# Fourteen probability blocks turned as float16 on TensorE, their low halves turned in pairs by one DMA, value products two to three steps later

## The reference, cut to what matters

```
q = x W_q;  k, v = text W_k, text W_v;  k_ip, v_ip = ip W_k_ip, ip W_v_ip
p = softmax(q k^T / 4)                        # per head, 112 x 371
text_out = p v
qsem = p text;  qsem = qsem / |qsem|          # 512 wide
sem = qsem . (ip / |ip|)
p_ip = softmax(q k_ip^T / 4 + 0.5 sem) * mask
out = (text_out + p_ip v_ip) W_out + b_out + x
```

## Time and profile before

| | |
|---|---|
| runs shown | 740.36 us median (739.94 to 740.94) |
| the profiled execution | 739.64 us, its span 736.4 us |
| PE busy | 715.9 us (97%) |
| DVE busy | 634.7 us (86%) |
| ACT busy | 558.0 us (76%) |
| POOL busy | 416.9 us (57%) |
| DMA queue of SP | 64.39 MB, 41.3% of 16 engines' time |
| granted TensorE clock | 0.993 of full speed over the span |

### The profile page before, as it was taken

How to read it: one execution, slowest core, us unless ns; L and a number is a source line. 1 busy time by engine, 2 the same in 40 slices (tenths; PEclk the granted TensorE clock), 3 DMA queues, 4 the chain that set the end, 5 groups by cost and what they waited for, 6 DMA issues and landing times.

```text
span 736.4 us, 22506 instructions
## 1 busy us (share of the span) xinstructions
PE 715.9 (97%) x7215; PEld 562.2 (76%) x7215; DVE 634.7 (86%) x1878; ACT 558.0 (76%) x1591; POOL 416.9 (57%) x513
## 2 busy tenths in 40 slices
PE   7798999999999999999999999999999999999897
PEld 5477788787887878788787878878777887877664
DVE  4488998989889898988989898898989889898984
ACT  5378787887878788787878878787787878777770
POOL 7244647456564645656565555656555565654653
PEclk9999999999999999999999999999999999999999
DMA  9665363452636335263534526353352635234000
GB/s 283 125 163 105 78 129 78 64 130 55 125 75 125 82 61 140 46 126 74 111 98 62 124 55 131 75 115 93 58 115 72 127 75 106 51 56 102 10 7 16
DMA packets 137058, 68.56 MB, mean 93 GB/s; under 512 B 77056, under 2 KB 136880, under 8 KB 136944
## 3 DMA queue, kind: packets, MB, share of 16 engines
q1 hardware_dynamic: 132368, 64.39, 41.3%
q10 hardware_dynamic: 4576, 2.74, 1.4%
HBM read 40.38 MB, written 15.24 MB: 76 GB/s over the span
## 4 chain that ended last, share of the span: by engine, by line
PE 90%; DVE 3%; ACT 1%; DMA 1%; issue 1%; ACTq 1%; POOL 0%; SPq 0%; POOLq 0%; DVEq 0%
PE ps_prep L634 18%; PE ps_gram L741 18%; PE ps_pT L724 13%; PE ps_gram L742 12%; PE ps_score L716 6%; PE ps_prep L695 5%; PE ps_val L750 4%; PE ps_val L751 2%; PE ps_prep L692 1%; PE ps_prep L778 1%; PE ps_prep L665 1%; PE ps_prep L667 1%; PE ps_prep L789 1%; DMA w_raw<-in_L_xattn_W_k_ip 1%; PE ps_prep L782 1%
## 5 line engine op out<-in xcount | busy, mean ns | idle before, releaser
L564 POOL TENSOR_TENSOR dual<-prob 128x371 f32<-128x371 f32 (+1 forms) x288 | 251.0, 872 | 290.6 <-ACT prob L941 290.6
L741 PE MATMUL ps_gram<-gram_hi,pT_hi 125*128 125x371 f16 (+1 forms) x864 | 272.4, 320 | 0.1
L742 PE MATMUL ps_gram<-gram_lo,pT_hi 125*128 125x371 f16 (+2 forms) x864 | 230.1, 267 | 0.0
L935 ACT ACTIVATE pT_hi<-ps_pT 125x384 f16<-125x384 f32 (+1 forms) x288 | 138.8, 482 | 115.0 <-PE ps_pT L724 107.1
L1116 DVE TENSOR_TENSOR pT_lo<-ps_pT,pT_hi 125x384 f16<-125x384 f32 (+1 forms) x288 | 155.2, 539 | 31.8 <-ACT pT_hi L935 27.3
L925 ACT ACTIVATE prob<-ps_score,low 128x371 f32<-128x371 f32 (+1 forms) x288 | 165.4, 574 | 20.5 <-DVE low L1111 15.3
L1111 DVE TENSOR_REDUCE low<-ps_score 128x1 f32<-128x371 f32 (+1 forms) x288 | 154.9, 538 | 16.8 <-PE ps_score L716 11.7
L1129 DVE CUSTOM_DVE_ANT_0 quad_junk<-ps_gram,dual 128x371 f32<-128x371 f32 (+1 forms) x288 | 153.1, 532 | 3.6 <-PE ps_gram L742 0.8
L750 PE MATMUL ps_val<-val,pT_hi 125*128 125x84 f16 (+3 forms) x864 | 152.3, 196 | 0.0
L941 ACT ACTIVATE prob<-prob 128x371 f16<-128x371 f32 (+1 forms) x288 | 151.5, 526 | 0.0
L724 PE MATMUL ps_pT<-ident,prob 128*125 128x128 f32 (+1 forms) x864 | 142.0, 273 | 7.7 <-ACT prob L925 4.0
(11 more groups left out here) (214 smaller groups left out, 1466.8 us busy)
## 6 DMA issues: line engine op xcount, KB each, us to landing
ctx_sb<-in_ctx_t SPq DMA_DIRECT2D x15, 750.0 KB, 4.9
w_raw<-k_bounce SPq DMA_DIRECT2D x32, 216.0 KB, 3.9
k_st<-k_bounce SPq DMA_DIRECT2D x28, 216.0 KB, 3.8
k_bounce<-k_hi SPq DMA_DIRECT2D x15, 288.0 KB, 4.3
k_bounce<-k_lo SPq DMA_DIRECT2D x15, 288.0 KB, 4.3
q_st<-q_bounce SPq DMA_DIRECT2D x60, 63.0 KB, 2.4
xt_sb<-in_x_t SPq DMA_DIRECT2D x16, 168.0 KB, 5.3
k_st<-k_hi SPq DMA_DIRECT2D x32, 84.0 KB, 3.2
```

Source lines behind the costliest of these rows:

```text
L564: nc.gpsimd.tensor_tensor(dual[0:r, t % 2, :], prob[0:r, g % 4, 0:TX], prob_16[0:r, t % 2, :], ALU.subtract).then_inc(s_dual, 1)
L741: nc.tensor.matmul(ps_gram[t % 2][:, 0:TX], hi, gh[0:TROWS[i], i, :], start=(i == 0), stop=False, skip_group_check=True)
L742: last = nc.tensor.matmul(ps_gram[t % 2][:, i * TC:TX], hi, gl[0:TROWS[i], i, i * TC:TX], start=False, stop=(i == NT - 1), skip_group_chec ...
```

## The change

Blocks 0 to 13 (t < `NBX`) are treated in another way; blocks 14 to 17 stay as they were, but for where they are stored.

1. ACT writes prob_16 = float16(prob), not half of it, one block earlier and ahead of `pT_hi` (block t+2 at the start of step t), into four slots.
2. PE turns `prob_16` with the float16 identity into a float16 view of `ps_pT`; ACT copies it out as `pT_hi`, now with five slots. DVE's `pT_lo` of these blocks is gone.
3. POOL makes `prob_lo` = prob - prob_16 as float16 in SBUF, unturned, for block t+2. For each pair of blocks SP issues one transposing DMA of 128x768 float16 (`turn_lo`) into `turned_lo`, three slots.
4. `dual` is made by POOL (prob + prob_lo) for odd blocks below 14 and for 14 to 17, and by DVE (2 prob - prob_16) for even blocks below 14.
5. Gram products of block t stay in step t. Value products are made in pairs: blocks 2q and 2q+1 in step 2q+3, blocks 12 to 15 in step 15, 16 and 17 in their own steps. The copies out of `ps_val`, the moving of the cut heads' rows (SP, steps 14 and 15 to 16 and 17) and the end of the batch before (two steps later) follow.

```
-            nc.gpsimd.tensor_tensor(dual[0:r, t % 2, :], prob[0:r, g % 4, 0:TX], prob_16[0:r, t % 2, :], ALU.subtract)
+VALUES_AT = {**{2 * q + 3: (2 * q, 2 * q + 1) for q in range(6)}, 15: (12, 13, 14, 15), 16: (16,), 17: (17,)}
+HI_SLOTS, X_SLOTS, LO_PAIRS, TURNED_PAIRS = 5, 4, 2, 3
+def dual_on_pool(t):
+    return t >= NBX or t % 2 == 1
+    def turn_lo(b, q):                                       # SP
+        n = pair(b, 2 * q)
+        sp.wait_ge(s_prob_lo, lows_to(b, 2 * q + 1))
+        if n >= TURNED_PAIRS:
+            past = n - TURNED_PAIRS
+            sp.wait_ge(s_val, NB * (past // PAIRS) + 2 * (past % PAIRS) + 2)
+        sp.dma_start_transpose(turned_lo[:, n % TURNED_PAIRS, :, :],
+                               prob_lo[:, n % LO_PAIRS, :, :, :].rearrange("s a c t -> s (a c t)")).then_inc(s_turned[n % TURNED_PAIRS], 16)
                 for t in range(NB):                          # SP's loop
+                    if t % 2 and t < NBX - 2:
+                        turn_lo(b, (t + 1) // 2)
+                    if prepare and t == NB - 1:
+                        turn_lo(b.next(), 0)
+    def low_probs(b, t):                                     # POOL
+        pool.wait_ge(s_prob_16, g + 1)
+        nc.gpsimd.tensor_tensor(prob_lo[:, n % LO_PAIRS, t % 2, :, 0:TC], chunks(prob[:, g % 4, :]), chunks(prob_16[:, g % X_SLOTS, :]), ALU.subtract)
     def transposes(b, t):                                    # PE
+        if t < NBX:
+            pe.wait_ge(s_prob_16, g + 1)
+            src, out_, unit = prob_16[0:r, g % X_SLOTS, :], ps_pT[:, :].bitcast(F16), ident_16
+    def value_products(b, t):                                # PE
+            if t % 2 == 0:
+                pe.wait_ge(s_turned[n % TURNED_PAIRS], 16 * (n // TURNED_PAIRS + 1))
+            lo = turned_lo[:, n % TURNED_PAIRS, t % 2 * NT:(t % 2 + 1) * NT, :]
-                    products(b, t)
+                    gram_products(b, t)
+                    for u in VALUES_AT.get(t, ()):
+                        value_products(b, u)
-            probs_lo(b, t + 1)                               # DVE
+            duals(b, t + 1)      # even blocks below 14; probs_lo for blocks 14 to 17
-MOVE_OUT_STEP, MOVE_IN_STEP = 14, 15
+MOVE_OUT_STEP, MOVE_IN_STEP = 16, 17
```

More of the change, by code:

```diff
@@ L107, in column, with duals_to, pair, lows_to @@
     return (t - GROUPS[group(t)][0]) * BW
+def dual_on_pool(t):
+    return t >= NBX or t % 2 == 1
+def duals_to(b, t):
+    own = sum(dual_on_pool(u) == dual_on_pool(t) for u in range(NB))
+    return own * b.n + sum(dual_on_pool(u) == dual_on_pool(t) for u in range(t + 1))
+def pair(b, t):
+    return PAIRS * b.n + t // 2
+def lows_to(b, t):
+    return NBX * b.n + t + 1
+def old_lows_to(b, t):
+    return (NB - NBX) * b.n + t - NBX + 1
+def block_of(g):
+    return Batch(g // NB, g // NB % 2, g // NB // 2), g % NB
 def place(a, k):
@@ L595, in end @@
                                             rsum[:, :].unsqueeze(2).to_broadcast([S, H, DH]), ALU.mult).then_inc(s_text_out, 1)
-            duals(Batch(0, 0, 0), 0)
+            for t in range(2):
+                low_probs(Batch(0, 0, 0), t)
             def body(b, prepare, turning, finishing):
                 for t in range(NB):
-                    if t + 1 < NB:
+                    if t + 2 < NBX:
+                        low_probs(b, t + 2)
+                    elif prepare and t + 2 >= NB:
+                        low_probs(b.next(), t + 2 - NB)
+                    if t + 1 < NB and dual_on_pool(t + 1):
                         duals(b, t + 1)
-                    elif prepare:
-                        duals(b.next(), 0)
                     if finishing:
@@ L732, in products @@
                     pe.wait_ge(s_prep_lo, NM * (b.n + 1))
-                pe.wait_ge(s_pT_lo, g + 1)
+                pe.wait_ge(s_pT_hi, g + 1)
                 reached(pe, s_quad, g - 1)
-                gh, gl, v = gram_hi[b.odd], gram_lo[b.odd], val[b.odd]
-                heads = slice(t, NB + t // XP + 1, NB + t // XP - t) if t < NBX else slice(t, t + 1)
-                o, n = column(t), 2 if t < NBX else 1
-                def gram_part(i):
-                    hi = pT_hi[0:TROWS[i], t % 2, i, :]
+                gh, gl = gram_hi[b.odd], gram_lo[b.odd]
+                for i in range(NT):
+                    hi = pT_hi[0:TROWS[i], g % HI_SLOTS, i, :]
                     nc.tensor.matmul(ps_gram[t % 2][:, 0:TX], hi, gh[0:TROWS[i], i, :], start=(i == 0), stop=False, skip_group_check=True)
@@ L743, in gram_part @@
                                             stop=(i == NT - 1), skip_group_check=True)
-                    if i == NT - 1:
-                        last.then_inc(s_gram, 1)
-                def val_part(i):
+                last.then_inc(s_gram, 1)
+            def value_products(b, t):
+                g, v = NB * b.n + t, val[b.odd]
+                if t == GROUPS[group(t)][0]:
+                    reached(pe, s_half, len(EVACS) * b.n + group(t))
+                if t == EVAC_BEHIND[2]:
+                    pe.wait_ge(s_half, len(EVACS) * b.n + 3)
+                if t < NBX:
+                    n = pair(b, t)
+                    if t % 2 == 0:
+                        pe.wait_ge(s_turned[n % TURNED_PAIRS], 16 * (n // TURNED_PAIRS + 1))
+                    lo = turned_lo[:, n % TURNED_PAIRS, t % 2 * NT:(t % 2 + 1) * NT, :]
+                else:
+                    pe.wait_ge(s_pT_lo, old_lows_to(b, t))
+                    lo = pT_lo[:, t - NBX, :, :]
+                heads = slice(t, NB + t // XP + 1, NB + t // XP - t) if t < NBX else slice(t, t + 1)
+                o, n = column(t), 2 if t < NBX else 1
+                out_ = ps_val[:, o:o + n * 2 * VW].rearrange("p (n w) -> p n w", w=2 * VW)
+                for i in range(NT):
@@ L752, in val_part @@
+                    last = nc.tensor.matmul(out_[:, :, 0:VW], lo[0:r, i, :], v[0:r, i, heads, 0:VW], start=False,
                                             stop=(i == NT - 1), skip_group_check=True)
-                    if i == NT - 1:
-                        last.then_inc(s_val, 1)
-                if t == GROUPS[group(t)][0]:
-                    for i in range(NT):
-                        gram_part(i)
-                    reached(pe, s_half, len(GROUPS) * b.n + group(t))
-                    for i in range(NT):
-                        val_part(i)
-                else:
-                    for i in range(NT):
-                        gram_part(i)
-                        val_part(i)
+                last.then_inc(s_val, 1)
@@ L1279, in _ @@
             nc.vector.tensor_copy(vip_rows[:, :], ps_prep[1][0:64, 64:64 + C]).then_inc(s_setup_ev, 1)
-            probs_lo(start, 0)
+            duals(start, 0)
             minimum(start, 2)
@@ L1295, in body @@
                     softly(t, 0)
-                    if t + 1 < NB:
+                    if NBX <= t + 1 < NB:
                         probs_lo(b, t + 1)
-                    elif prepare:
-                        probs_lo(b.next(), 0)
+                    elif t + 1 < NB and not dual_on_pool(t + 1):
+                        duals(b, t + 1)
+                    elif t + 1 == NB and prepare:
+                        duals(b.next(), 0)
                     if prepare and t in TAKE_STEP:
```

136 lines of the change are left out of this document (86 added, 50 removed).

## The result

The changed kernel takes 867.75 us, the median of four runs (866.31 to 868.95), against 740.15 for the kernel before on the same chip: a ratio of 1.172 (95% interval 1.170 to 1.175). I had forecast 773, with a range of 724 to 845. The direction is right, the size is not.

The account below looks back on a forecast made before the run. PE's own instructions were taken to bound the kernel, 43.08 us a batch. From 739.6, minus 31.4 for the turning, plus 64.5 for waits on transposing DMAs, gave 772.7, so 773 us with the median's 0.7; range 724 to 845.

Parts of the forecast that it names:

- DVE, ACT and POOL costed at nothing: Per batch DVE 34.6 us, POOL 31.2, ACT's counts unchanged, all under PE's 41.1, so no cost was added.
- dear rival: Transposing DMAs on SP cost much more, four ahead of the second wait: 812 to 864 us; chance 0.22.
- T: Time SP needs to issue one transposing DMA: taken as 1.0 us, ends 0.34 and 2.2.
- Turning, - 31.4: On PE, float16 transposes replace float32 in 14 of 18 sets a batch: 224 x 0.14 = 31.4 us saved.
- The rival that it saves nothing: On PE, float16 transposes wait or load weights as long as before: 804 us; chance 0.07.
- Place and form of the wait: PE waits once a batch, at the first value product of step 9 or 13, for a DMA into turned_lo.
- Its size, 4.3 a batch: PE's wait for late transposing DMAs, 4.1 us in step 9 or 4.5 in step 13: 15 x 4.3 = 64.5.
- 2T + L - 1.1: PE's wait in step 9 for blocks 6 and 7, from issue time and landing time: 4.1 us.
- L: Time from a transposing DMA's issue to its landing: taken as 3.2 us, ends 1.8 and 4.3.
- The second wait (blocks 10 and 11): PE in step 13 waits for their transposing DMA: 4.5 us, the earlier wait included.
- the sign that the text named for it: Waits of PE for ACT, DVE or POOL, costed at nothing, would show the forecast wrong.
- the waits don't add up: Within a batch, after one wait PE is later for everything else and SP isn't, so 4.3 us in all.

Follow-up runs that it names:

- e13_no_lows: The changed kernel without transposing DMAs and waits for them, POOL making low halves of four elements a row instead of 375; 707.52 us (0.955).
- e3_no_turn: The changed kernel without its transposing DMAs and the waits for them, values of blocks 0 to 13 using the high half twice; 731.47 us (0.987).
- e8_slots: The changed kernel with three slots of prob_lo in place of two; 846.11 us (1.143).
- e14_turn_no_lows: The changed kernel with k's stores in step 5, way back in 7, cut heads in 10, three prob_lo slots, POOL's low halves cut to four elements; 732.57 us.
- e2_order: The changed kernel with k's eight cut-head loads and k's way back from DRAM placed further behind on SP (steps 8 and 9); 785.48 us (1.057).
- e12_fprob_dve: The changed kernel with k's stores in step 5, way back in 7, cut heads in 10, three prob_lo slots, fprob on POOL, block 10's dual on DVE; 762.86 us.

## Why the prediction was wrong, by its steps

The result lies 95 us above the forecast. By its own steps, two failed in kind: DVE, ACT and POOL costed at nothing (24 us, measured without DMAs), and what a wait sets off in the other engines, not in the sum at all (38 us more). A third was mis-sized, the wait itself (36 us). The turning gave 3 us more than forecast. That the dear rival's upper end, 864, comes near 867.75 is luck: it had T = 2.2 and a second wait, and neither is there.

- **Turning, - 31.4**: right. e13_no_lows is 34 us below the kernel before (741.6 on that chip), its batch 41.11 against the 41.12 (43.08 - 1.96) that follow from the earlier trace rows. The rival that it saves nothing is out.
- **Place and form of the wait**: right. Step 9, once a batch, on the first value product, in the 15 batches that were reckoned with. PE asks 21.3 us behind step 0 (forecast 21.2).
- **Its size, 4.3 a batch**: mis-sized: 6.6 on average, 7.1 in the batch shown, 100.3 in all, where 64.5 stood. T is 1.25, not 1.0. The issue begins at 23.6, not 22.1: two transposes ahead at 1.25 are 0.5 of that, q's and k's own DMAs, which I took from the kernel before, the other 1.0. The landing took 4.8, not 3.2, and lay beyond the upper end I had written down (4.3, the 288 KB store). With T = 1.25 and L = 4.8 the formula 2T + L - 1.1 gives 6.2, and 7.2 with the 1.0.
- **The second wait (blocks 10 and 11)**: absent; PE was late by then, as the text said of waits in one batch.
- **DVE, ACT and POOL at nothing**: this step failed, and the sign that the text named for it came, PE's waits for DVE (`val` and `fprob`: 26.4 us, against 1.3 before). The busy sums were near (DVE 34.5 where POOL is out of the way, against 34.6; POOL 32.4, against 31.2), and the conclusion "all stay under PE's 41.1" did not follow. The change replaces `pT_lo`, which reads PSUM and SBUF, by a dual that reads SBUF twice, and gives POOL 14 low halves a batch for 7 duals, all of them long and all reading SBUF. I priced the dual by the row of 0.533, an operation that reads PSUM. That cost 24 us without any DMA (e3_no_turn against e13_no_lows).
- **What a wait sets off**: this step failed too. I wrote that PE is later for everything else and that the waits don't add up. But POOL stands still too (9.1 us for a slot), then catches up without a gap, and DVE is shut out during that: the 3.54 us above. Adding up: 740.2 - 34 + 24 + 100 = 830; 38 us remain. They and the 24 can't be kept apart in the changed kernel, where both are DVE late in step 11. Most of the 62 lies between the landing and step 12: 8.6 us a batch there, against 6.5 in e3_no_turn and 5.02 in e13_no_lows, and 15 x 3.6 is 54. e8_slots, which takes most of POOL's catching up away, gives back 22, 6 of them in the wait itself; the 2.1 a batch that it keeps in this stretch are PE at half clock.
- **The clock**: I did not consider it. It fell to 0.50 for some 10 us a batch. In the changed kernel, where POOL and DVE set the stretch behind the wait, it cost nothing on top; with DVE on time (e8_slots) it is 31 us.
- **Seven DMAs on SP**: in my text they delay one another. Whether they also delay k's way to the next batch is open: of the 25 us of e14_turn_no_lows 10 are the moved order at the start, and the other 15 are not separated.

The Trainium skill, SBUF — State Buffer, section Who interferes with whom, states the rule that I should have weighed: a VectorE instruction with both inputs in SBUF contends with a GpSimd instruction that reads SBUF, and one with at most one SBUF input, outside the two-port modes, does not. The traces agree in kind: the dual beside POOL took 0.53 us and up to 1.5 in the changed kernel (3.4 in e2_order), and the minimum and the gram reduction, which read PSUM, 0.53 to 0.54 on average in every kernel here. Of the two-port modes this page of the Trainium skill says that whoever issues first holds the pair of ports for the whole instruction. Here DVE waited for more than one of POOL's: in the changed kernel it got in at none of the boundaries between 326.58 and 329.09, only when POOL's run ended at 329.97. In e3_no_turn the dual of 1.39 us, from 359.44 to 360.83, got in at POOL's first gap, 0.18 us that end at 360.61:

```profile
358.73 0.90 POOL L612 TENSOR_TENSOR prob_lo<-prob 128x375 f16<-128x375 f32 x1
359.59 0.84 POOL L565 TENSOR_TENSOR text_lo<-ctx_sb,text_hi 128x375 f16<-128x375 f32 x1
360.61 0.97 POOL L612 TENSOR_TENSOR prob_lo<-prob 128x375 f16<-128x375 f32 x1 [0.18 <-ACT prob L1014]
```

But a gap is not needed. In e12_fprob_dve a dual passed over three boundaries (335.71, 336.53, 337.39) and ended at 338.65, 0.44 behind the fourth (338.21), inside a run without a gap; the `text_lo` that POOL began there took 1.20 in place of the 0.85 above. Which boundary lets DVE in, no run here shows:

```profile
335.49 3.16 DVE L1218 SCALAR_TENSOR_TENSOR dual<-prob 128x371 f32<-128x371 f32 x1
```
```profile
338.21 1.20 POOL L571 TENSOR_TENSOR text_lo<-ctx_sb,text_hi 128x375 f16<-128x375 f32 x1
339.37 0.88 POOL L629 TENSOR_TENSOR dual<-prob,prob_lo 128x375 f32<-128x375 f32 x1
```
